# A two-layer graph network on one core: the second layer's first batch prepared inside the first layer, its second batch projected later

## What is computed

```python
# layer 0: 4 heads of 64, keys in 8 chunks of 256 nodes, a softmax in each chunk
h = relu(layernorm(x))
q, k, v = h @ Wq.T + bq, h @ Wk.T + bk, h @ Wv.T + bv      # split in heads
s = clip(q @ k.T / 8, -10, 10);  s = where(mask == 0, -10, s)
o = sum over chunks of softmax(s in the chunk) @ v
x = x + (layernorm(o @ Wo.T + bo + h) * gamma + beta)
# layer 1: graph attention with 4 heads of 64
h = relu(layernorm(x));  Wh = h @ W                          # per head
e = leaky_relu(Wh_i . a1 + Wh_j . a2, 0.2), masked by adj
x = x + elu(softmax(e) @ Wh)
```

## Time and profile before

| | |
|---|---|
| median of 3 runs | 4598.11 us |
| lowest and highest run | 4597.84, 4601.86 us |
| the profiled execution, its own time | 4597.83 us |
| its span (first to last instruction) | 4596.0 us |
| TensorE busy | 4386.1 us, 95% |
| VectorE busy | 3494.4 us, 76% |
| GpSimd busy | 3009.0 us, 65% |
| ScalarE busy | 2987.9 us, 65% |
| mean granted TensorE clock | 0.983 |

### The profile page before, as it was taken

How to read it: one execution, slowest core, us unless ns; L and a number is a source line. 1 busy time by engine, 2 the same in 40 slices (tenths; PEclk the granted TensorE clock), 3 DMA queues, 4 the chain that set the end, 5 groups by cost and what they waited for, 6 DMA issues and landing times. The chain is left out here.

```text
span 4596.0 us, 84237 instructions
## 1 busy us (share of the span) xinstructions
PE 4386.1 (95%) x34312; PEld 2615.8 (57%) x34312; DVE 3494.4 (76%) x4562; ACT 2987.9 (65%) x3498; POOL 3009.0 (65%) x2422
## 2 busy tenths in 40 slices
PE   7999999999999999999999999389999999999997
PEld 3334334334334334333333433279999999999997
DVE  5875775775776776776687577478898989889895
ACT  4664664664665565556466466188887888888885
POOL 5685685675775676577477477356665757667585
PEclk9999999999999999999999999689999999999999
DMA  6001000000001000001000000111121212112011
GB/s 197 10 10 37 10 10 28 19 10 28 19 10 28 19 10 28 10 10 33 15 10 19 10 10 19 35 47 50 56 68 41 75 32 70 54 47 82 29 59 42
DMA packets 126979, 160.88 MB, mean 35 GB/s; under 512 B 8832, under 2 KB 109184, under 8 KB 126592
## 3 DMA queue, kind: packets, MB, share of 16 engines
q1 hardware_dynamic: 126592, 155.49, 10.7%
HBM read 121.64 MB, written 33.83 MB: 34 GB/s over the span
## 5 line engine op out<-in xcount | busy, mean ns | idle before, releaser
L583 ACT ACTIVATE e_sb<-e_sb 128x1024 f32<-128x1024 f32 x1024 | 1082.4, 1058 | 835.7 <-DVE e_sb L684 798.3
L684 DVE SCALAR_TENSOR_TENSOR e_sb<-psS,mask 128x1024 f32<-128x1024 f32 x1024 | 1202.9, 1216 | 348.0 <-PE psS L815 341.5
L1414 PE MATMUL psA<-xy,ring_p 128*128 128x195 bf16 x8192 | 1405.1, 248 | 13.6 <-DVE red L1294 13.6
L1414 PE MATMUL psA<-xy,ring_s 128*128 128x195 bf16 x8192 | 1404.6, 249 | 0.0
L414 POOL TENSOR_TENSOR e_sum<-e_sb 128x1024 f32<-128x1024 f32 x384 | 918.5, 2392 | 325.5 <-ACT e_sb L583 219.0
L1214 ACT ACTIVATE ring_s<-eiB,ejb 128x1024 int8<-128x1024 f32 x1024 | 1089.8, 1137 | 9.5 <-PE psA L1414 9.5
L815 PE MATMUL psS<-qT,kT 64*128 64x512 f32 x4096 | 1042.2, 613 | 3.0 <-DVE e_sb L684 2.9
L828 PE MATMUL psN<-e_sb,v_sb 128*32 128x512 f32 x8192 | 985.0, 598 | 0.0
L1414 PEld LDWEIGHTS psA<-xy,ring_p 128*128 128x128 fp8e4 x8192 | 801.5, 98 | 19.9 <-DVE red L1294 17.0
L1414 PEld LDWEIGHTS psA<-xy,ring_s 128*128 128x128 fp8e4 x8192 | 800.5, 98 | 8.6 <-issue 0.3
L431 POOL TENSOR_TENSOR ctxT<-ctxT,num 128x512 f32<-128x512 f32 x384 | 488.1, 1277 | 456.2 <-DVE num L659 349.9
(11 more groups left out here) (120 smaller groups left out, 4158.0 us busy)
## 6 DMA issues: line engine op xcount, KB each, us to landing
eiB<-ei_between SPq DMA_DIRECT2D x64, 512.0 KB, 4.1
xin<-x SPq DMA_DIRECT2D x32, 512.0 KB, 3.9
xr<-x SPq DMA_DIRECT2D x32, 512.0 KB, 4.8
x_between<-hy SPq DMA_DIRECT2D x32, 512.0 KB, 3.2
xin<-x_between SPq DMA_DIRECT2D x32, 512.0 KB, 5.6
xo<-x_between SPq DMA_DIRECT2D x32, 512.0 KB, 4.5
out<-o_sb SPq DMA_DIRECT2D x32, 512.0 KB, 5.3
xr<-adjT SPq DMA_DIRECT2D x24, 512.0 KB, 4.1
```

What stands on the lines that cost most here:

```text
L583: act.activation(e_sb[:, n % ES], e_sb[:, n % ES], ACT.Exp, scale=SCALE).then_inc(exp_done, 1)
L684: dve.scalar_tensor_tensor(out=e_sb[:, n % ES], in0=psS[:, s % 2], scalar=-CLIP_RAW, in1=mask[:, kb, cols][:, None, :].to_broadcast([P, 2, ...
L1414: ins = pe.matmul(psA[:, i % BANKS, br * PARTS * XW:(br + 1) * PARTS * XW], part[:, n % RING, k, tt * TW + j * P:tt * TW + (j + 1) * P], x ...
```

## The change

Four things are done.

1. **Preparation of layer 1's batch 0** moves into layer 0. The load of W, a1 and a2 goes behind the adjacency's loads, the folding of a1 and a2 into W is done at group 2 of batch 0. In the stretch between batches 6 and 7 the kernel puts 8 more groups (GAPX), and in it (and under the projections of batch 7) the four tiles of x_between's batch 0 are loaded into layer 0's xin as soon as a tile's transposes are done, normalized, transposed into psN, copied to hT, multiplied with W into psS and copied to wh. The edge terms, the maximum, the transpose of ei and the exponentials are placed at groups 6 to 41 of batch 7. Buffers that both layers use are allocated outside of both (class Between).
2. **The mask's reduction to the edge bit** is placed at the end of VectorE's stream in layer 0.
3. **Layer 1** begins at slot FIRST = 48 - 64 - 1 = -17, and the weighting of batch 0, head 0 is at the slots where it was.
4. **Layer 1's batch 1** has its tiles at slots -2 + 10 t in place of -8 + 12 t: its first norm is at slot -1 (before: -7), its first transposes at slot 1 (before: -5), its first product at slot 5 (before: -1).

The diff, cut to its core (tables of constants moved up unchanged, and the many lines that only take a buffer or semaphore from `two`, are left out):

```diff
+GAPX = 8
+NORM1_AT, TURN1_AT, WH1_AT = (6, 10, 14, 18), (18, 19, 23, 27), (19, 23, 27, 31)
+RS1_AT, EJ1_AT, EIT1_AT, CEN1_AT, EXP1_AT, XQV1_AT = (6, 7, 8, 9), 22, 35, 38, 40, 41
+WALL_AT = 2
...
         def alive(b, k):
-            return [(b, k)] + ([(b - 1, k + GROUPS + GAPG)] if b and k + GROUPS + GAPG < TAILG else [])
+            before = k + GROUPS + gap(b - 1)
+            return [(b, k)] + ([(b - 1, before)] if b and before < TAILG else [])
+
+        def gap(b):
+            return GAPG + (GAPX if b == nb - 2 else 0)
...
         # sync engine, layer 0
             load_adjacency()
+            for c in range(FH):
+                sp.dma_start(w_all[:, c, :, 0:D], w[c * P:(c + 1) * P, :, :]).then_inc(w_in, 16)
+            sp.dma_start(a_rows[:, 0], a1.partition_broadcast(P)).then_inc(w_in, 16)
+            sp.dma_start(a_rows[:, 1], a2.partition_broadcast(P)).then_inc(w_in, 16)
...
+                    if t == T - 2 and b + 2 == nb:
+                        for i in range(2):
+                            sp.wait_ge(x1_out[i], T // 2 * 16)
+                        for u in range(T):
+                            sp.wait_ge(tr_done, (nb - 1) * T + u + 1)
+                            if u >= 2:
+                                sp.wait_ge(h1_done, u - 1)
+                            sp.dma_start(xin[:, u], tile_of(x1_v, 0, u)).then_inc(x1_in[u % 2], 16)
+                    if t == 0 and b + 1 == nb:
+                        exchange_max()
+                        store_ei()
                     store(b, t)
...
         # scalar engine, layer 0
+            def second_layer(v):
+                for t in range(T):
+                    if v == TURN1_AT[t] + (1 if t else 0):
+                        act.wait_ge(tr1_done, t + 1)
+                        act.activation(hT[:, t % 2], psN[:, :, :], ACT.Copy).then_inc(hT1_done, 1)
+                    for i in range(2):
+                        if v == WH1_AT[t] + 1 + i:
+                            act.wait_ge(wh_proj, 2 * t + i + 1)
+                            act.activation(wh[:, TB * t + 2 * i].rearrange("p h e -> p (h e)"),
+                                           psS[:, i, 0, 0:H * W1], ACT.Copy).then_inc(wh_done[0], 1)
...
         # vector engine, layer 0
+            def weights():
+                dve.wait_ge(w_in, 64)
+                wlink = linker(dve, w_chain, 0)
+                for c in range(FH):
+                    for part in range(2):
+                        wlink(dve.tensor_tensor(wa, w_all[:, c, :, 0:D], a_rows[:, part], ALU.mult))
+                        wlink(dve.tensor_reduce(w_all[:, c, :, D + part], wa, AX.X, ALU.add))
+
+            def second_layer(v):
+                for t in range(T):
+                    if v == NORM1_AT[t]:
+                        dve.wait_ge(x1_in[t % 2], 16 * (t // 2 + 1))
+                        ln_moments(dve, link, mv1[:, TB * t:TB * t + TB], stats, tmp1[:, 0:TB], lambda j: xin[:, t, j, :], TB)
+                        for j in range(TB):
+                            ins = dve.tensor_scalar(xin[:, t, j, :], xin[:, t, j, :], mv1[:, TB * t + j, 0:1], 0.0,
+                                                    ALU.subtract, ALU.max)
+                        ins.then_inc(h1_done, 1)
...
+            def one_bit_masks():
+                dve.wait_ge(edge_done, 1)
+                for k in range(0, BLK, 4):
+                    dve.tensor_tensor(adj_w[:, k:k + 4], adj_w[:, k:k + 4],
+                                      edge_w[:, :, None].to_broadcast([P, 4, N // 4]), ALU.bitwise_and)
...
+                    if b == 0 and k == WALL_AT:
+                        weights()
+            dve.memset(edge[:, :], EDGE).then_inc(edge_done, 1)
+            one_bit_masks()
...
         # tensor engine, layer 0
+                if s == 0 and b == nb - 1:
+                    for i in range(2):
+                        pe.wait_ge(wh_done[i], 2 * T)
...
+            def second_layer(v):
+                for t in range(T):
+                    for i in range(2):
+                        if v == WH1_AT[t] + i:
+                            if i == 0:
+                                pe.wait_ge(hT1_done, t + 1)
+                            if t:
+                                for k in range(2):
+                                    pe.wait_ge(wh_done[k], 2 * (t - 1) + i + 1)
...
+                            for k in range(2):
+                                nodes = slice((2 * i + k) * P, (2 * i + k + 1) * P)
+                                ins = product(psS[:, i, k, 0:H * W1], lambda c: hT[:, t % 2, c, nodes],
+                                              lambda c: w_all[:, c].rearrange("p h e -> p (h e)"))
+                            ins.then_inc(wh_proj, 1)
+                for t in range(T):
+                    if v == TURN1_AT[t]:
+                        pe.wait_ge(h1_done, t + 1)
+                        for c in range(FH):
+                            for j in range(TB):
+                                ins = pe.transpose(psN[:, c, j * P:(j + 1) * P], xin[:, t, j, c * P:(c + 1) * P], ident[:, :])
+                        ins.then_inc(tr1_done, 1)
...
         # layer 1
-        FIRST, LAST = PREP_FROM - SLOTS, nb * SLOTS + 24
+        FIRST, LAST = MULT_W[0] - SLOTS - 1, nb * SLOTS + 24
...
         def tile_at(g, at):
-            return [(b, (s - LN0 - at) // LN_STEP) for b, s in preparing(g)
-                    if 0 <= s - LN0 - at < T * LN_STEP and (s - LN0 - at) % LN_STEP == 0]
+            found = []
+            for b, s in preparing(g):
+                first, step = (-2, 10) if b == 1 else (LN0, LN_STEP)
+                if 0 <= s - first - at < T * step and (s - first - at) % step == 0:
+                    found.append((b, (s - first - at) // step))
+            return found
...
         # vector engine, layer 1
-            dve.memset(edge[:, :], EDGE).then_inc(edge_done, 1)
-            dve.wait_ge(edge_done, 1)
-            for k in range(0, BLK, 4):
-
-                ins = dve.tensor_tensor(adj_w[:, k:k + 4], adj_w[:, k:k + 4],
-                                        edge_w[:, :, None].to_broadcast([P, 4, N // 4]), ALU.bitwise_and)
-            ins.then_inc(adj_done, 1)
-            dve.wait_ge(const_in, 64)
-            link = linker(dve, w_chain, 0)
```

More of the change, by code:

```diff
@@ L118, in linker @@
     return link
-def layer0(nc, mask, x, adjT, wqT, wkT, wvT, woT, bq, bk, bv, bo, gamma, beta, x1, nb):
+W1 = D + 2
+XW = D + 1
+PARTS = 3
+KC = 4
+KCH = BLK // KC
+TT = 2
+TH = T // TT
+SW = TT * TW
+SU = H * TH
+U = SU * TT
+SLOTS = U * KCH
+RING = 2 * KCH
+BANKS = 6
+ALPHA = 0.2
+SHIFT = 60.0
+EDGE = 0x40
+SIGN_LEAD = 10
+MASK_LEAD = 8
+LN0, LN_STEP = -8, 12
+H_AT1, TR_AT1, HT_AT1, WH_AT1, COPY_AT1 = 1, 3, 5, (7, 11), (9, 13)
+RS_W = 41
+EJ_W = 42
+EIT_W, EIC_W = 43, 44
+CEN_W, EXP_W, XQV_W = 46, 47, 48
@@ new lines, with __init__, sb, sem @@
+MULT_W = (48, 1, 14, 30)
+HI_W = (51, 3, 18, 34)
+REST_W = (52, 4, 19, 35)
+MID_W = (54, 6, 21, 37)
+LO_W = (55, 7, 22, 38)
+ELU_W = tuple(SLOTS - 6 + KCH * t for t in range(T))
+PREP_FROM = -20
+GAPX = 8
+NORM1_AT, TURN1_AT, WH1_AT = (6, 10, 14, 18), (18, 19, 23, 27), (19, 23, 27, 31)
+RS1_AT, EJ1_AT, EIT1_AT, CEN1_AT, EXP1_AT, XQV1_AT = (6, 7, 8, 9), 22, 35, 38, 40, 41
+WALL_AT = 2
+class Between:
+    def __init__(self, nc, ctx, nb):
+        def sb(name, shape, dt=F32):
+            return ctx.enter_context(nc.sbuf_tensor(name, shape, dt))
+        def sem(name):
+            return ctx.enter_context(nc.semaphore(name))
+        self.mask = sb("mask", [P, BLK, N], I8)
+        self.ident = sb("ident", [P, P])
+        self.w_all = sb("w_all", [P, FH, H, W1])
+        self.wh0 = sb("wh0", [P, BLK, H, W1])
+        self.ejb = sb("ejb", [P, 2, BLK, H])
+        self.xq = sb("xq", [P, 2, BLK, H])
+        self.xqv = sb("xqv", [P, 2, BLK, H])
+        self.cq = sb("cq", [P, 2, 2, BLK, H])
+        self.ei_d = nc.dram_tensor("ei_between", [nb, H, N], F32).ap()
+        self.mx_d = nc.dram_tensor("max_between", [nb, P * H], F32).ap()
+        self.x_in = [sem(f"x1_in{i}") for i in range(2)]
+        self.h_done = sem("h1_done")
+        self.tr_done = sem("tr1_done")
+        self.hT_done = sem("hT1_done")
+        self.wh_proj = sem("wh_proj")
+        self.wh_done = [sem(f"wh_done{i}") for i in range(2)]
+        self.ei_done = sem("ei_done")
+        self.mxp_done = sem("mxp_done")
+        self.mx_out = sem("mx_out")
+        self.mx_in = sem("mx_in")
+        self.eiT_done = sem("eiT_done")
+        self.eis_done = sem("eis_done")
+        self.ei_out = sem("ei_out")
+        self.d_done = sem("d_done")
+        self.q_done = sem("q1_done")
+        self.xqv_done = sem("xqv_done")
@@ L123, in layer0 @@
+def layer0(nc, two, x, adjT, wqT, wkT, wvT, woT, bq, bk, bv, bo, gamma, beta, w, a1, a2, x1, nb):
     with ExitStack() as ctx:
@@ L131, in sem @@
             return ctx.enter_context(nc.semaphore(name))
```

(33 more changed lines are left out.)

185 lines of the change are left out of this document (92 added, 93 removed).

## The result

| | before | after |
|---|---|---|
| median of 4 runs each | 4599.98 us | 4571.85 us |
| lowest and highest run | 4597.84, 4602.28 us | 4571.35, 4573.90 us |
| the profiled execution, its own time | 4597.83 us | 4572.13 us |
| its span | 4596.0 us | 4570.3 us |
| mean granted TensorE clock | 0.983 | 0.986 |

The ratio is 0.994, interval [0.9922, 0.9957]. The changed kernel is faster, and 4571.85 us lies in the forecast range of 4555 to 4585, 3.9 above the forecast of 4568. The kernel before has four runs here, one more than the three on which the forecast stood.

What follows compares the result with a forecast made beforehand. Layer 0 was taken as bound by TensorE, the boundary by a 64.7 us chain where nothing overlaps. 4597.8 - 64.4 + 21.5 + 1.0 + 1.5 + 8.5 + 2.0 = 4567.9, rounded 4568 us; range 4555 to 4585.

Steps and rivals of the forecast that it cites:

- Added, 1: Between batches 6 and 7: eight more groups, bound by TensorE, add 18.5 us of work plus 3 of waits, 21.5 us.
- Removed: Head of layer 1: all 64.7 us of preparation leave, 0.3 us stays before the first weighting; net -64.4 us.
- Batch 7: Layer 0's last batch: the edge terms spread over 36 groups, mostly hidden by VectorE's idle quarter, add 1.5 us.
- The folding: Batch 0 of layer 0: folding the attention vectors into the weights takes 3.7 us, VectorE's slack leaves 1.0 us.
- The ANDs: End of layer 0: four mask ANDs each block one small GpSimd instruction, adding 8.5 us.
- Rival A: End of layer 0: the mask ANDs are free, small GpSimd instructions slip between them; 4559 us, chance 0.18.
- The second batch: Start of layer 1: batch 1's later preparation gives back the masks' products' earlier start; +2.0 us, between -11 and +5.
- Rival B: Between batches 6 and 7: nothing overlaps, each tile's steps run in sequence, 37 us in place of 21.5; 4584, chance 0.13.
- C: Between batches 6 and 7: TensorE's clock falls, doubling 33 us of projections and 18.5 of new work; 4620, chance 0.03.
- D: Start of layer 1: batch 0's terms aren't ready, their transfers queue with stores, 11.4 us still paid; 4579, chance 0.03.

## Why the prediction was right, point by point

The total was right, and so was the mechanism of each of the large terms. The step that was off most is "Added, 1", the stretch.

- **Removed, -64.4 (measured -64.7).** The load of eiB hid behind the weighting (the first Sign comes 5.2 us behind p, as before); layer 1's turn costs 3.42 us as it did.
- **The stretch, +21.5 (measured +24.8).** "That is 4.0 + 14.5 = 18.5 us" and "I take 3 in all" were both close. What the sum left out is that the tail of batch 6 came into the new groups: the two output projections (1.99 and 1.89 us; before they stood behind batch 7's first scores, at 2581.55 and 2588.10) and two broadcasts, some 4.5 us of TensorE. 18.5 + 4.5 make the 23.0 of busy time, and 1.8 are waits. The prediction saw that ("the batch after starts lighter"), but used it for the lower end of the range only, and the batch after didn't show it, for the reason in the next point.
- **Batch 7, +1.5 (measured +1.0).** Right in sum by two errors. The 4.5 us that left it should have made it -4.5; against that stand TensorE's waits for normalizations (9.9 us in 11 places against 7.0 in 9) and for the inverse (0.7 more), and 1.8 us of the last tile's second output projection, which ran at the lower clock (3.78 us against 1.99). In all TensorE waits 21.8 us there in place of 18.9 and is busy 313.7 in place of 315.6. That the change caused the 1.8 us isn't shown (see the last point on the hardware). The group named, "the group with the maximum and the centring", is where the longest wait is, 2.21 us; but spreading its work brought nothing.
- **The folding, +1.0 (measured +2.7).** Mis-sized: "VectorE has slack in a batch" is true of the mean and not of a group. The folding held VectorE for 6.1 us in one piece (82.13 to 88.2), and TensorE waited for the clip behind it, 2.39 us. Part of the length is the meeting that the prediction priced for the ANDs but not here. In the kernel before, with GpSimd idle, the same eight instructions took 3.6 us (2931.42 to 2935.03) and each product 0.41 to 0.43; here the products took 0.69 to 2.02 us, the longest beside a sum of GpSimd (VectorE's timeline first, then GpSimd's):

```profile
84.58 2.02 DVE L887 TENSOR_TENSOR ctxT<-w_all,r_f 128x256 f32<-128x256 f32 x1
...
83.78 2.53 POOL L546 TENSOR_TENSOR e_sum<-e_sb 128x1024 f32<-128x1024 f32 x1
```

- **The ANDs, +8.5 (measured +7.8).** The four blocked instructions took 2.35, 2.09, 2.12 and 2.12 us: one for each AND, in the place named. The term was 4 x (2.25 - 0.1), which is 8.6 and was written as 8.5; with the 0.2 us that such an instruction takes alone it would have been 8.2. Rival A is refuted, and the experiment with the operand in PSUM shows the cause by taking it away. The rule of the Trainium skill (SBUF — State Buffer, Who interferes with whom) that a VectorE instruction with two SBUF inputs and a GpSimd instruction that reads SBUF exclude each other agrees with both: blocked with two SBUF inputs, free with one.
- **The second batch, +2.0 (measured +1.5 in the ramp, +0.8 behind it).** The walk's early marks were right to the us: first product p + 15.3 (said 15.3), slots 0 and 1 to p + 23.4 (said 24), the wait of 5.9 us for the norm (said 5), the transpose at p + 29.3 (said 29.4). Slots 2 and 3 ended at about p + 38 (said 39 to 42; of the 12.33 us for four slots the last two, at the upper clock, have 5.4) and slot 15 at p + 75.1 (said 76 to 79). But it was set "against 75.5 before at the same state of work", and that state has one product more, 1.8 us, which the walk left out. Two small errors cancel: like for like it is p + 76.9 against p + 75.45. What it missed is that the same kernel with batch 1 at its old places would be quicker still: set against that, the move costs about 2.5 us.
- **Rival B** is refuted by the stretch (24.8 us, not 37, no wait but the two named) and by its products taken twice, **C** by the granted clock of 1.00 in both of its parts, **D** by line 1403, which waits only for its own stream's turn.

## What to carry to other kernels

Slack that an average shows is not slack where a block of new work is put: price an addition by the longest piece in which it holds its engine against the time until the next engine wants a result. When work moves past the end of a stage, move its neighbours in the sum too: what leaves the next stage enters this one. And before giving an idle engine something to do, ask whose instructions it will hold up: here four ANDs on an idle VectorE cost 7.8 us on GpSimd's path, and one operand in another memory made them free.

## What the runs showed of the hardware

**Operands.** Four ANDs of 128 x 2048 words cost the same on VectorE from SBUF and PSUM (8.89 and 8.88 us), but only with both inputs in SBUF did a GpSimd instruction of 0.2 us take 2.1 beside each.

**Single-input instructions too.** Line 926 of the kernel with the centring spread has one SBUF input and took 2.29 us in place of 0.2, until 0.06 us after GpSimd's sum beside it had ended. The Trainium skill (SBUF — State Buffer, Who interferes with whom) says that such an instruction can enter a mode in which it needs the shared ports too. I didn't test whether it is that here.

**A granted clock that falls in some executions only.** In batch 7 TensorE waits 2.2 us for a normalization at 2782. In the changed kernel the clock stays at its upper level (2.4 GHz). With the operand in PSUM, the same wait in the same place was followed by the lower one (1.2 GHz): the seven matmuls of line 1038 (1040 here) behind it took 3.55 us in place of 1.98. Busy by stretch, the changed kernel first, then that one:

```profile
2768.00:2790.00 22.00, 19.79 (x139) 7.34 (x141) 17.31 (x21) 11.28 (x17) 16.35 (x10) 1.00 0.01 1
```

```profile
2768.00:2790.00 22.00, 19.77 (x130) 7.69 (x126) 17.14 (x21) 11.85 (x18) 15.03 (x10) 0.92 0.01 1
```

Of ten profiled executions with this wait, three had the drop (0.92, with 338.5 to 338.8 us for batch 7) and seven not (1.00; 337.1 where the rest of the batch is unedited). Neither of the two without the wait had it. Two are too few to call the wait its cause.

**The last tile's second projection.** Before the change it ran at the upper level (1.99 us), the first at the lower (3.78), both behind the same chain of broadcasts; after it, both ran at the lower (3.78 us each), and in all eleven experiments both took 3.65 to 3.78 us. What TensorE did before them is the same in both traces to 0.01 us over the last nine broadcasts. The granted clock rises at different times there. In the kernel before it rose 4.4 us before the end of the last aggregate, in time for that projection. In eight of the twelve changed kernels it rose 1.5 to 2.2 us before that end, when the projection was through or nearly so, and in four, the changed kernel among them, not at all before it. There is one trace of the kernel before, so whether the edit or the execution decides stays open.
